# First cross attention of a transformer block: its output product as three products of rounded halves

## The reference, cut to what matters

```
x = x + _L0_xattn_ref(_layernorm(x), ctx_768, w_q, b_q, w_k, b_k, w_v, b_v, w_o, b_o)

def _L0_xattn_ref(x, context, ...):
    q, k, v = x @ w_q + b_q, context @ w_k + b_k, context @ w_v + b_v     # 16 heads of 16
    weights = softmax(q k^T / sqrt(16))
    out = (weights v) back to (B, 112, 256)
    return out @ w_o + b_o
```

## Time and profile before

| | us |
|---|---|
| median of 3 runs | 2076.18 (2075.4 to 2077.92) |
| the profiled execution, its own time | 2077.91 |
| span of the profiled execution | 2076.1 |
| mean granted TensorE clock | 0.976 of full |

### The profile page before, as it was taken

One profiled execution on the slowest core, in us unless ns is written; L12 is line 12 of the kernel. 1 busy time (PEld: TensorE's weight loads), 2 busy tenths in 40 slices (PEclk: granted clock), 3 DMA queues, 4 the chain that ended last, 5 costly groups with the idle time before them and its releaser, 6 DMA issues.

```text
span 2076.1 us, 59362 instructions
## 1 busy us (share of the span) xinstructions
PE 1971.5 (95%) x20383; PEld 1636.4 (79%) x20384; DVE 1356.3 (65%) x3358; ACT 1082.9 (52%) x2530; POOL 924.2 (45%) x1554
## 2 busy tenths in 40 slices
PE   7999999998889999799999999889999999999995
PEld 5888888886677777599999999767777778778784
DVE  6777777775488888643333333348878788787875
ACT  2555555554467777332222332356666666666672
POOL 4544545452377777500000000256666666666651
PEclk9999999999799999899999999979999999999998
DMA  8232232330440000211111111311111111110100
GB/s 224 85 100 93 86 108 83 110 86 2 164 159 27 22 22 24 83 33 35 35 38 38 35 35 35 98 29 29 33 30 40 28 38 32 35 35 28 40 19 9
DMA packets 98072, 118.73 MB, mean 57 GB/s; under 512 B 9442, under 2 KB 90466, under 8 KB 97890
## 3 DMA queue, kind: packets, MB, share of 16 engines
q1 hardware_dynamic: 91874, 103.32, 16.2%
q0 software_dynamic: 6144, 14.69, 2.4%
HBM read 67.26 MB, written 50.72 MB: 57 GB/s over the span
## 4 chain that ended last, share of the span: by engine, by line
PE 84%; DVE 6%; issue 5%; ACT 2%; POOL 1%; DMA 1%; DVEq 0%; POOLq 0%; ACTq 0%; SPq 0%
PE ps_proj L258 19%; PE ps_quad L1433 11%; PE ps_out L1448 10%; PE ps_quad L578 5%; PE ps_quad L136 4%; PE ps_out L158 4%; PE ps_turned L147 4%; PE ps_out L586 3%; PE ps_proj L1863 3%; PE ps_proj L1842 3%; DVE s_negmax L1030 2%; PE ps_proj L662 2%; PE ps_turned L564 2%; PE ps_out L1202 1%; PE ps_proj L1152 1%
## 5 line engine op out<-in xcount | busy, mean ns | idle before, releaser
L1352 ACT ACTIVATE e_act_T<-ps_quad,fc_b 128x128 f32<-128x128 f32 x504 | 137.2, 384 | 313.3 <-PE ps_quad L1433 313.3
L1433 PEld LDWEIGHTS ps_quad<-e_xT,e_w_now 128*128 128x128 f32 x2016 | 234.6, 192 | 7.7 <-DVE e_xT L1392 3.9
L1433 PE MATMUL ps_quad<-e_xT,e_w_now 128*128 128x128 f32 x2016 | 235.7, 275 | 3.4 <-DVE e_xT L1392 3.4
L1448 PE MATMUL ps_out<-w,e_act_T 128*128 x1008 | 228.1, 379 | 0.8 <-DVE e_y L1400 0.8
L413 ACT ACTIVATE a_probsT<-ps_quad 125x1792 f32<-125x1792 f32 x96 | 160.0, 1666 | 101.5 <-PE ps_quad L578 101.5
L1448 PEld LDWEIGHTS ps_out<-w,e_act_T 128*128 128x128 f32 x1008 | 186.6, 190 | 24.0 <-issue 1.2
L1581 POOL MEMSET c_cT<- 128x2 f32 x2 | 0.1, 102 | 461.0 <-DMA c_wk<-in_L_xattn_Wk 461.0
L1389 DVE COPY e_w_now<-w 128x2048 f32 (+1 forms) x63 | 77.3, 1227 | 191.8 <-PE ps_quad L1433 188.5
L1577 POOL TENSOR_TENSOR c_kL<-c_kT,c_kH 128x376 fp32r<-128x376 f32 x128 | 126.3, 987 | 155.1 <-ACT c_kH L1646 154.4
L178 DVE TENSOR_SCALAR c_probs<-c_probs,c_recip 112x375 f32<-112x375 f32 x256 | 155.9, 649 | 4.6
L1641 ACT ACTIVATE c_kT<-ps_proj 128x376 f32<-128x376 f32 x128 | 62.0, 484 | 175.6 <-PE ps_proj L258 175.6
(11 more groups left out here) (316 smaller groups left out, 5375.2 us busy)
## 6 DMA issues: line engine op xcount, KB each, us to landing
slots<-a_zeros SPq DMA_DIRECT2D x60, 512.0 KB, 5.0
a_cT<-in_ctx_t SPq DMA_DIRECT2D x32, 375.0 KB, 3.6
c_cT<-in_ctx_t SPq DMA_DIRECT2D x32, 375.0 KB, 3.2
w<-in_fc_t SPq DMA_DIRECT2D x2, 4096.0 KB, 19.3
w<-in_fc_t SPq DMA_DIRECT2D x8, 1024.0 KB, 12.2
e_xg<-slots SPq DMA_DIRECT2D x63, 128.0 KB, 2.0
slots<-e_y SPq DMA_DIRECT2D x63, 128.0 KB, 1.7
out<-c_fo SPq DMA_DIRECT2D x32, 112.0 KB, 1.9
```

Of the source, the lines that this page charges most:

```text
L1352: last = act.activation(act_T[par][:, c * TILE:(c + 1) * TILE], hidden[par][:, c // 4, (c % 4) * TILE:(c % 4 + 1) * TILE], ACT.Gelu, bias= ...
L1433: last = pe.matmul(hidden[par][:, c // 4, (c % 4) * TILE:(c % 4 + 1) * TILE], w1_now[:, k, c * 128:(c + 1) * 128], xT[par][:, k, :], start ...
L1448: last = pe.matmul(y_ps[:, 0:D], act_T[1 - par][:, c * TILE:(c + 1) * TILE], w2[:, bass.ds(e, 1), c, :].rearrange("p a d -> p (a d)"), sta ...
```

## The change

The two fp32 products become six fp32r products, the three terms of `split_terms` for each half of the 256 rows of `wo`. This needs four new buffers: `oH`, `oL` (128 x 224) and `woH`, `woL` (128 x 512).

```diff
+        oH, oL = (sb(n, [128, 2, T], F32R) for n in ("oH", "oL"))
+        woH, woL = (sb(n, [128, 2, D], F32R) for n in ("woH", "woL"))
...
@@ pool, step: behind qL of nxt, ahead of context_high(third)
+                    if exists(b):
+                        pool.wait_ge(o_high, b + 1)
+                        wait(pool, op_mm, b)
+                        pool.tensor_tensor(oL[:, :, :], oT2[:, :, :], oH[:, :, :], ALU.subtract).then_inc(o_low, 1)
                     if exists(third):
                         context_high(third, 1 - par)
                         context_low(third, 1 - par)
@@ act, step
                         act.wait_ge(oT2_mm, b + 1)
+                        wait(act, o_low, b)
                         act.activation(oT2[:, :, :].rearrange("p k t -> p (k t)"), outs[:, 0:HALF], ACT.Copy).then_inc(oT2_ready, 1)
                     if exists(nxt):
                         shift_copy(nxt, 1)
+                    if exists(b):
+                        act.wait_ge(oT2_ready, b + 1)
+                        wait(act, op_mm, b)
+                        act.activation(oH[:, :, :], oT2[:, :, :], ACT.Copy).then_inc(o_high, 1)
+                    if exists(nxt):
                         exp(nxt, 0)
                         exp(nxt, 1)
+                    if isinstance(b, int) and b == -2:
+                        act.wait_ge(wo_in, 16)
+                        act.activation(woH[:, :, :], wo[:, :, :], ACT.Copy).then_inc(wo_high, 1)
@@ dve, step
+                    if isinstance(b, int) and b == -2:
+                        dve.wait_ge(wo_high, 1)
+                        dve.tensor_tensor(woL[:, :, :], wo[:, :, :], woH[:, :, :], ALU.subtract).then_inc(wo_split, 1)
@@ pe, step
-                        pe.wait_ge(wo_in, 16)
-                        pe.wait_ge(oT2_ready, b + 1)
-                        for k in range(2):
-                            last = pe.matmul(outs[0:T, D:2 * D], oT2[:, k, :], wo[:, k, :], start=(k == 0), stop=(k == 1))
-                        last.then_inc(op_mm, 1)
+                        if isinstance(b, int) and b == 0:
+                            pe.wait_ge(wo_split, 1)
+                        pe.wait_ge(o_low, b + 1)
+                        chain(pe, outs[0:T, D:2 * D], [term for k in range(2) for term in split_terms((oH[:, k, :], oL[:, k, :]), (woH[:, k, :], woL[:, k, :]))])\
+                            .then_inc(op_mm, 1)
```

More of the change, by code:

```diff
@@ L296, in cross_first @@
         oT, oT2 = sb("oT", [128, 4, T]), sb("oT2", [128, 2, T])
+        oH, oL = (sb(n, [128, 2, T], F32R) for n in ("oH", "oL"))
+        woH, woL = (sb(n, [128, 2, D], F32R) for n in ("woH", "woL"))
+        wo_high, wo_split, o_high, o_low = sem("wo_high"), sem("wo_split"), sem("o_high"), sem("o_low")
         recip, on, o = sb("recip", [T, H]), sb("on", [T, D]), sb("o", [T, D])
```

## The result

The changed kernel takes 2134.61 us, the median of 4 runs (2131.50 to 2137.22), against 2076.30 before (4 runs, 2075.40 to 2077.92). The ratio is 1.0279, with a 95% interval of 1.0261 to 1.0297: 58.3 us slower. The profiled execution has a span of 2135.3 and an own time of 2137.22. The forecast was 2122 with a range of 2108 to 2138: right in its sign, inside its range, and 12.6 us too low.

A forecast was written before the change was run, and what follows sets the result against it. POOL's written order was taken to bound: 1.37 us queue delay plus 0.2 meetings less 0.02, 1.55 in each of 29 steps, 45.0 us; edges +0.5, PE and ACT 0: 45.5, so 2122 us, range 2108 to 2138.

The forecast's parts named there:

- What bounds the kernel: PE's output product lies beside ACT's exponential, so its 0.05 to 0.2 us gain shows at most 0.15 a batch; booked 0.
- ACT's part: The extra 128 x 224 rounding to `oH` on ACT ends before the exponential starts, 0.2 us to spare; cost 0.
- the sign that I had set: Prediction counts as wrong if ACT's exponential starts later than 1.1 us after ACT's copy.
- POOL's chain: On POOL, context and norm queue behind `oL`'s wait for `oH`; PE's last plain scores start 1.37 us later in a step.
- The meetings on the port: POOL and DVE share a port: `qH` meets the context's subtractions, `kH` meets `oL`; 0.1 us each, step 1.55 in all.
- The rival in which `qH` waits for the whole norm: Port keeps DVE's `qH` away until POOL's norm is done; last scores 2.0 us late, 58 us, 2134 in all; 8%.
- The meeting of `kH` and `oL`: DVE's `kH` rounding runs across the start of POOL's `oL` and may hold it up by up to 0.17 us; 0.1 taken.
- The edges: First and last batches: making the halves of `wo` costs 0, the last three steps +0.5 us in all.
- The clock: PE's clock falls after its stall in each step, 1.5 us each, another 43 us, 2165; 9%; a few steps within range.
- the rival on the port: DVE's `qH` kept from the port until POOL's whole norm is done: 2134 us, 8%; range had to include it.
- the cover holds: DVE's norm is still in time and PE's saving shows, 0.1 to 0.2 us a step, 5 us faster, 2071; 3%.
- no effect: POOL's delay is just covered by unseen slack, nothing measurable: 2076 within 4 us; 4%.

The follow-up runs named there:

- e5: Changed kernel with only PE's six products; ACT writes its copy as `oH`, which stands in for `oL`, no rounding or subtraction for it: 2075.32 us, 0.9992 of before.
- e3: Changed kernel with PE repeating the second value projection twice (ten matmuls) in each full step just before its stall: ratio 1.0251 to before; run again 2124.41 us, 1.0229.
- the repeats: The kernel before and the changed kernel run once more, unchanged, on one chip: before 0.9997 against itself, changed 2135.19 us, ratio 1.0285.
- e4: Changed kernel with POOL's subtraction for `oL` done twice, the second into a buffer nobody reads: ratio 1.0407 to before.
- e7: Changed kernel with both PE's ten extra value-projection matmuls per full step and POOL's second subtraction for `oL`: 2138.76 us, ratio 1.0305 to before.
- e2: Changed kernel with POOL's norm moved directly behind `oL`, and the third batch's context halves behind the norm: ratio 1.0072 to before.
- e1: Changed kernel with POOL doing the third batch's context halves ahead of `oL`, the norm staying behind it: ratio 1.0040 to before; run again 2077.62 us, 1.0004.

## Why the prediction was right, and where its size was off

**What bounds the kernel: right.** PE's busy share and its 0.87 in the chain promised a gain; e5, which has that gain alone, is 0.9992 of before. I booked 0 and named 0.15 us a step as the most that can show; 0.05 did. The output product itself was said to take 0.70, and that was too low. From the first to the last start it is 0.66, and with one more pitch of 0.12 it is 0.78, nearer to the upper bound of 0.82.

**ACT's part: right.** `oH` ends at +0.88 as predicted (+0.87), and the exponential waits for PE. But the sign that I had set, wrong if the exponential starts later than 1.1 us after the copy, was a bad one: it starts at +1.16 in every second step, and does so in the kernel before too. I had read one batch, with +1.09, and called all alike, although they come in two kinds by turns.

**POOL's chain: right, link by link.** `oL` started at +0.96 (0.94 predicted) and took 0.66 to 0.70 (0.67). The subtractions of the context ended at +4.85 (4.65), the norm at +5.63 (5.49), and the last plain scores started at +6.99 (7.06 with both meetings). In the steps at full clock this gave 1.35 and 1.61 by turns, 1.50 in the mean of e3, where 1.55 was predicted: 43.6 us for 45.0. That the two differ I had not foreseen. In the longer ones, but for the very first of them, the first weight load behind the last plain scores, which opens the next step of PE's program, comes after 0.30 us in which it waited for nothing that the profile shows, and PE then waits 0.30 for the exponential; the shorter ones have neither:

```profile
311.81 0.19 PEld L597 LDWEIGHTS ps_quad<-a_shift,a_ones 32*125 32x125 f32 x4 [0.30 <-issue]
...
314.81 0.43 PE L583 MATMUL ps_quad<-a_kH,a_qH 32*112 32x376 f32 x4 [0.30 <-ACT a_probsT L420]
```

These are the steps that end with the loop's jump. That the jump is the cause is my reading, which no run tested.

**The meetings on the port: right in sum, wrong in how.** I had `qH` wait for both subtractions and end near +4.9, and then hold up the norm. It ended at +4.02, and held up the second subtraction instead (1.13 for 0.99), so that the pair took 2.08 for 1.94. This 0.14 is what I had put at 0.1. The error was in my reading of the earlier trace rows. They show the pair as one row, and taken alone the second subtraction starts before `qH` does, which begins at 35.85:

```profile
35.74 1.00 POOL L376 TENSOR_TENSOR a_kL<-a_kT,a_kH 128x376 fp32r<-128x376 f32 x1
```

So `qH` never waited for two operations there. It waited for the one that was running, and ended 0.25 behind its end. In the changed kernel it starts in the first subtraction, which ends at 324.96, and ends at 325.22, 0.26 behind it. With the same reading the prediction would have had `qH` end at +3.95. The Trainium skill, page "SBUF — State Buffer", section "SBUF: two separate sides", says that whichever of the two starts first has the shared pair for a whole instruction. By that rule `qH` takes the pair when the first subtraction gives it back. The new trace agrees.

The rival in which `qH` waits for the whole norm, 2134, fell with it, although its number lies close to the result: e3 has no falls of the clock and a mean step of 16.6, where that rival needs 17.1. The meeting of `kH` and `oL`, also put at 0.1, was 0.04 at most (0.66 or 0.70).

**The edges: right, as far as can be measured.** I had +0.5 for them. From the thirtieth copy to the last are 29.58 us, before 29.20; in the repeats 28.82 and 28.89.

**The clock: the term that was mis-sized.** I had put it at 0 in the forecast, gave 9% to a fall in each step, and wrote that a fall in a few steps only stays within the range. The mechanism was the right one, in eleven of 29 steps. A step with a fall cost 15.0 / 11.5 = 1.3 us in the mean of the two runs, 1.2 for each 3.4 us at half clock, where I had estimated 1.5 for 3 us. The step of the working that failed was "against it: here the stall lies between full matmuls": that did not protect it. The forecast should have held a term of some 1.5 us for a part of the steps. 43.6 and 15.0 stand against 45.0 and 0: the miss of 12.6 us is this term less 1.4 on the queue, to within a microsecond.

That the result lies in the range is in part luck. My forecast's own range, 1.2 to 1.8 us a step, was 2111 to 2129, and 2134.61 lies outside it. The range was drawn up to 2138 to take in the rival on the port, which did not happen, and that room took up the clock.

Of the rivals, *the cover holds* is refuted by DVE's wait for POOL of 1.66, and *no effect* by the ratio. Of the signs that I had named, POOL's wait for `oH`, DVE's for POOL, PE's for the maximum and a `qH` of about 1 us are in the rows. Of the steps of 16.5 to 16.8 the mean is (16.6 in e3), and they come as 16.38 and 16.81.

## What to carry to other kernels

An engine that works in written order pays for a wait with everything queued behind it, not with the operation that waits. Before inserting one, look for the next item in that queue which another engine wants soon, and put first what is ready and slack: here the same operations in another order cost nothing. And when a change makes PE stand still in a stage where it had not, price the clock as well as the wait. A filler of useless matmuls is a cheap way to tell the two apart. And before a row with xN is used for who waited for whom, read its N instructions one by one.

## What the runs showed of the hardware that I had not expected

- **Equal stalls, unequal clock.** In the changed kernel PE waits 1.1 to 1.3 us in every full step, but the granted clock falls to half behind 11 or 12 of the 29, for 3.4 us each, in one for 6.8. Waits of 1.9 to 2.0 us (e4) made it fall behind 10. Ten extra matmuls of 0.12 us pitch ahead of the remaining wait kept it at 1.00 throughout, even with the second subtraction (e7). Which of the stalls makes it fall I can't say.
- **DVE waits for the one instruction that POOL is in, and gets its turn before the next.** A rounding to `qH` that takes 0.39 to 0.40 alone ended 0.25 or 0.26 behind the end of the POOL instruction in which it had started, in each of four places looked at: 36.99 behind 36.74 (before, with the earlier trace rows), 325.22 behind 324.96 (after), 284.07 behind 283.82 (e2, beside a rounding) and 313.68 behind 313.43 (e4, beside a rounding). How much it cost, 0.13 or 0.74, hung on where in that instruction it began. The norm's application in e2 ended 0.15 behind a subtraction.
- **One chip was slower in one stage.** The kernel before took 2120.26 on one chip and medians of 2075.65 to 2076.35 on the others. In e1, which was profiled on both, self attention took 345.1 us there and 304.4 elsewhere, two batches mostly in 22.0 to 24.6 us against 19.7. From 640 to 740 us of it DVE's idle time had 12.4 us of waiting for what the profile calls remote, of which the other profile has none, and the granted clock was 0.97 against 1.00. What lies behind it is open. Kernels that are compared should share a chip.
